# GpSimd adds the two key halves of the weights before the sums' product, and the residual one tick later

## The reference, cut to what matters

```python
x = x + _L2_attn_ref(_layernorm(x, axis=-1), ...)
qkv = data @ W_qkv + b_qkv
scores = jnp.einsum('nqhd,nkhd->nhqk', q, k)
attention = jax.nn.softmax(scores / jnp.sqrt(jnp.float32(HD)), axis=3)
out = jnp.einsum('nhql,nlhd->nqhd', attention, v).reshape(n, l, DIM)
return out @ W_out + b_out
```

## Time and profile before

| | before |
|---|---|
| median of 3 runs | 2783.32 us (2780.84 to 2787.41) |
| profiled execution | 2796.33 us |
| its span | 2794.7 us |
| PE busy | 2456.9 us, 88% |
| DVE busy | 1694.2 us, 61% |
| ACT busy | 1488.0 us, 53% |
| POOL busy | 1457.4 us, 52% |

### The profile page before, as it was taken

How to read it: one execution, slowest core, us unless ns; L and a number is a source line. 1 busy time by engine, 2 the same in 40 slices (tenths; PEclk the granted TensorE clock), 3 DMA queues, 4 the chain that set the end, 5 groups by cost and what they waited for, 6 DMA issues and landing times. The chain is left out here.

```text
span 2794.7 us, 62868 instructions
## 1 busy us (share of the span) xinstructions
PE 2456.9 (88%) x24585; PEld 1891.2 (68%) x24585; DVE 1694.2 (61%) x4435; ACT 1488.0 (53%) x3177; POOL 1457.4 (52%) x2282
## 2 busy tenths in 40 slices
PE   4999999999988688889998999999999676778855
PEld 3888888888876455557777777777777564445533
DVE  4677777777657477745444666666665215555557
ACT  3666666666644467744444555555555224555631
POOL 4787777777766444434332344444444126554454
PEclk9999999999999699999999999999999897999975
DMA  3790000000000100000000000000000440000000
GB/s 108 237 329 16 2 2 2 2 2 2 2 2 1 50 2 2 2 1 22 0 1 3 4 4 4 6 6 4 5 5 5 153 141 16 7 7 3 1 1 30
DMA packets 23255, 83.14 MB, mean 30 GB/s; under 512 B 4113, under 2 KB 11026, under 8 KB 21938
## 3 DMA queue, kind: packets, MB, share of 16 engines
q1 hardware_dynamic: 19810, 71.90, 7.9%
q0 software_dynamic: 3152, 7.21, 0.8%
HBM read 71.89 MB, written 46.79 MB: 42 GB/s over the span
## 5 line engine op out<-in xcount | busy, mean ns | idle before, releaser
L825 POOL TENSOR_TENSOR XR<-XR,T 128x256 f32<-128x256 f32 x512 | 375.9, 734 | 441.8 <-DVE T L708 411.7
L2416 PE MATMUL ps<-P,V 128*64 128x256 f32 (+3 forms) x4096 | 338.6, 353 | 14.4 <-DVE O L1270 12.3
L589 ACT ACTIVATE P<-ps 128x384 f32<-128x384 f32 (+1 forms) x512 | 250.7, 542 | 187.6 <-PE ps L2416 187.1
L1260 DVE TENSOR_REDUCE qa<-ps 128x2 fp32r<-128x512 f32 x256 | 176.4, 689 | 211.6 <-PE ps L2416 210.8
L1188 ACT ACTIVATE P<-ps 128x768 f32<-128x768 f32 x256 | 207.8, 812 | 147.9 <-PE ps L2416 146.6
L2416 PEld LDWEIGHTS ps<-P,V 128*64 128x64 f32 (+1 forms) x4096 | 187.1, 125 | 125.5 <-issue 25.6
L2416 PE MATMUL ps<-mk,identb 128*128 128x256 bf16 (+1 forms) x1024 | 199.5, 297 | 68.2 <-DVE qa L1261 65.3
L719 DVE TENSOR_REDUCE sm<-ps 128x2 f32<-128x512 f32 (+1 forms) x256 | 130.7, 552 | 179.2 <-PE ps L2416 178.4
L1350 POOL TENSOR_SCALAR_AFFINE_SELECT P<-P 128x512 f32<-128x512 f32 x256 | 163.2, 638 | 137.4 <-ACT P L1188 137.3
L836 POOL TENSOR_TENSOR ss<-ss,nhalf 128x16 f32<-128x16 f32 x64 | 187.8, 2935 | 5.3
L2416 PE MATMUL ps<-QH,KH 64*128 64x256 f32 (+1 forms) x1024 | 165.4, 314 | 8.6 <-DVE QL L677 0.6
(11 more groups left out here) (312 smaller groups left out, 7361.4 us busy)
## 6 DMA issues: line engine op xcount, KB each, us to landing
rows_i<-in_zero SPq DMA_DIRECT2D x16, 1208.0 KB, 31.6
rows_o<-in_zero SPq DMA_DIRECT2D x16, 1208.0 KB, 80.2
w<-in_m_w SPq DMA_DIRECT2D x23, 578.0 KB, 4.0
zt<-rows_i SPq DMA_DIRECT2D x23, 128.0 KB, 3.1
rows_o<-yo POOLq DMA_DIRECT2D x23, 128.0 KB, 3.9
stg<-in_t_w SPq DMA_DIRECT2D x11, 256.0 KB, 2.7
XR<-in_x SPq DMA_DIRECT2D x4, 512.0 KB, 8.5
out<-XR SPq DMA_DIRECT2D x8, 256.0 KB, 2.0
```

Source lines behind the costliest of these rows:

```text
L589: e.activation(self.P[at % 6][:, :], K.ps.ap("st", s, g, h)[:, 0:self.w], ACT.Exp, bias=0.0, scale=1.0 if kind == 0 else 0.125).then_inc(K ...
L825: p = po.e.tensor_tensor(x, x, self.T[g % 2][:, par, pr], ALU.add)
L1260: e.tensor_reduce(nm[:, 1], ps[:, :, 0:256], X, ALU.max, negate=True)
L2416: return self.te.matmul(o, l, r, start=start, stop=True, skip_group_check=True)
```

## The change

In kind 2, POOL adds the second half of the columns of each head's `P` to the first half, into one of eight new tiles `PS` of 128x256, two heads a tick, in the ticks of `st`. The product with ones then runs over `PS`: four products a unit in place of eight, each clearing its own strip. PE waits for the semaphore `halved` between the weighted values and the sums; ACT may write a buffer of `P` again when the weighted values are done and POOL has halved it, where it waited for the sums. `pool_sum` moves from k = 13 to k = 14, and `unit` from 14 to 15, so a unit has one more part and `Dispatch` starts one tick later. Kind 0 keeps its work.

```diff
-            first, last, unit = 6, 5, 14
+            first, last, unit = 6, 5, 15
...
+            self.PS = [sb(f"PS{s}_{i}", [128, 256], F32) for i in range(8)]
+            self.halved = K.sem(f"halved{s}")
...
-        for kt, q, c, w in self.blocks():
+        if kind == 2:
+            pe.wait_ge(self.halved, 4 * g + 4)
             for h in range(4):
-                p = K.acc(sm[32 * h:32 * h + 32, q:q + w], self.one[:, 0:32], P[h][:, c:c + w],
-                          start=kind == 2 and kt == 0)
+                p = K.acc(sm[32 * h:32 * h + 32, 0:256], self.one[:, 0:32], self.PS[(4 * g + h) % 8][:, :], start=True)
...
-                    ac.wait_ge(*K.ps.filled("sm", s, (at - 6) // 4))
+                    ac.wait_ge(*K.ps.filled("sm" if kind == 0 else "pv", s, (at - 6) // 4))
+                    if kind == 2:
+                        ac.wait_ge(self.halved, at - 5)
...
-                if self.part("out", k) is not None:
+                n = self.part("st", k)
+                if n is not None and self.kind == 2:
+                    self.pool_halve(po, 4 * a[0] + a[1], n)
+                if k == self.tk["out"] + (self.kind == 2):
                     self.pool_sum(po, *a)
...
+    def pool_halve(self, po, g, n):
+        K, s = self.K, self.s
+        for h in (2 * n, 2 * n + 1):
+            at = 4 * g + h
+            if at >= 8:
+                po.wait_ge(*K.ps.filled("sm", s, g - 2))
+            po.wait_ge(*K.ps.read("st", s, g, h))
+            P = self.P[at % 6]
+            po.e.tensor_tensor(self.PS[at % 8][:, :], P[:, 0:256], P[:, 256:512], ALU.add).then_inc(self.halved, 1)
```

More of the change, by code:

```diff
@@ L461, in pe_pv @@
         p.then_inc(K.ps.full_of("pv", s, g), 1)
-        for kt, q, c, w in self.blocks():
+        if kind == 2:
+            pe.wait_ge(self.halved, 4 * g + 4)
             for h in range(4):
-                p = K.acc(sm[32 * h:32 * h + 32, q:q + w], self.one[:, 0:32], P[h][:, c:c + w],
-                          start=kind == 2 and kt == 0)
+                p = K.acc(sm[32 * h:32 * h + 32, 0:256], self.one[:, 0:32], self.PS[(4 * g + h) % 8][:, :], start=True)
+        for kt, q, c, w in self.blocks() if kind == 0 else ():
+            for h in range(4):
+                p = K.acc(sm[32 * h:32 * h + 32, q:q + w], self.one[:, 0:32], P[h][:, c:c + w])
         p.then_inc(K.ps.full_of("sm", s, g), 1)
```

## The result

| | before | after |
|---|---|---|
| median of the runs | 2782.88 us (4 runs) | 2845.51 us (4 runs, 2841.1 to 2852.5) |
| profiled execution | 2796.33 us | 2848.57 us |
| stage, first product to the places of its last scatter | 662.1 us | 722.9 us |
| one sequence: gated unit, the next, two plain | 10.27 + 10.35 + 9.68 + 9.68 = 39.97 us | 14.81 + 10.94 + 9.30 + 9.31 = 44.37 us |

The gated unit is the one in four that carries a `prep` and a `Dispatch`. The ratio is 1.0221 [1.0207, 1.0235]: 62.6 us slower, where +34.8 was forecast. The stage itself is 60.8 us longer, so the loss lies in it. (The two profiled executions differ by only 52.2 us, because the one of before lies 13 us above its median.) The periods of the units are distances between the starts of their weighted values; 14 sequences x (44.37 - 39.97) = 61.6 us (the first of them is 0.8 shorter).

The account below looks back on a forecast made before the run. PE was taken to bound the kernel, busy 69.09 of 70 us. Terms: -27.5 + 60.5 + 1.8 = +34.8 us on the median 2783.3, forecast 2818 us; range 2782 to 2850.

Parts of the forecast that it names:

- What PE saves: PE's sums in each unit: 8 instructions in place of 16, 0.43 us less, 27.5 us over 64 units.
- The halving's cover: POOL's halvings, 0.79 us each, are hidden behind PE's weighted values of 1.88 us; no wait taken before the sums.
- The bank: Second scores product waits for banks read by QL and the reciprocal, late behind POOL's adds: PE loses 2.36 us, 14 times.
- The transposes of zd: PE, ready at 11.98 us, waits until 13.94 for DVE's zd, which now stands behind T, nm and KL.
- this unit loses 4.32 us: Unit where `prep` and `Dispatch` meet: next weighted values start at 14.16 us, not 9.84; 14 times, 60.5 us.
- the clock falls too: Rival: PE's granted clock falls after its waits, 1.62 us lost each; one at each of 14 places gives 2841; chance 0.18.
- b = 14: The sequence whose `Dispatch` meets no `prep`: adds early, only zd late, 1.8 us lost.
- the likeliest case: Whole kernel from 2808 to 2828 us, with each of the 14 losses between 3.6 and 5.0 us.
- one wait alone: Rival: only the bank's wait, net +5.5 us, 2789; or only zd's, net about -0.5 us, 2783; chance 0.13.

Follow-up runs that it names:

- work in both waits: Against the kernel after, in 14 sequences PE computes the values' product three times ahead of zd's transposes and the output product twice ahead of the bank wait; ratio 1.0169.

## Why the prediction was right in its direction and too low

- **What PE saves: right.** The sums take 0.64 us for 1.07. Plain units take 9.30 us for the forecast 9.25: scores wait 0.19 us for ACT in about half of the units, which the forecast had left out.
- **The halving's cover: right in this kernel, for less reason than given.** 731 ns each, where 0.79 us with its wait was taken from the add, and no wait for it. The argument looked at the exponentials alone; the kernel with the halving alone shows that the adds' place in POOL's queue decides it.
- **The bank: right.** Counted from the weighted values, the adds were to end at 6.52 us, QL to start at 7.45, the scores at 8.59; they did at 6.50, 7.35 and 8.41. The wait is 2.30 us, 2.36 was forecast.
- **The transposes of zd: right in place, too small.** KL was to end at 13.2 us and ended at 13.15. Then zd was priced at 0.59 from the earlier trace rows. In the moved place POOL runs adds of 128x256 beside it, and it takes 1.00: this is the first mis-sized term, 0.41 us a sequence, about 6 us. In the step "this unit loses 4.32 us", the operation kept the price of its old neighbours.
- **The clock: the second mis-sized term, and the larger one.** The forecast took no fall and gave "the clock falls too" a chance of 0.18. That rival is what happened, in addition to the forecast: 1.48 us a sequence was measured against the 1.62 that the rival had from the earlier trace rows. The choice rested on one row in which a wait of 2.03 us was followed by a clock of 1.00. That row excludes nothing: with the adds ahead of the roots this very wait has a fall behind it, and in the kernel with the early gate, waits of one length, 2.3 us, had one in 9 of 14 sequences.

The sum: a sequence was to take 39.97 - 4 x 0.43 + 4.32 = 42.57 us. Without falls it takes 42.89 (work in both waits): 0.41 more in the gated unit, as much as zd takes more, and 0.10 less in the other three. With falls it takes 44.37. The excess of 1.80 us x 14 is 25 us. For b = 14 the gated unit took 12.53 us where it took 9.90 before, 2.63 more where -0.43 + 1.8 = 1.37 was forecast, another 1.3 (the 15th wait for zd, 2.8 us). Together that is 26 of the 28 us between the forecast of 2818 and 2845.5. The measured time lies above the likeliest case, 2808 to 2828, and a little above the 2841 of the rival with one fall a sequence; it is inside the range because the range was drawn up to a fall at most places, not because the sum held.

The rival on the other side, one wait alone, has its two halves measured. With the wait for zd alone (the adds ahead of the roots) the ratio is 1.0066, where 2783 of 2783 was forecast; with the bank's alone (the gate a tick earlier) it is 1.0108, where 2789 was. In both the larger part of the difference is not the clock: without a fall a sequence takes 40.83 us where 40.05 follows from the forecast, and 41.89 where 40.61 does. The two instructions of zd take 1.65 and 1.24 us there, in place of 0.59, and what stands behind zd is late with it; no run separates the two. The falls add 6.0 us in all to the one kernel and 2.2 us to the other.

What stays open is when the clock falls. Both waits gave 14 falls in 14 sequences (after), the bank's alone 9 in 14, the bank's with that of zd cut to 1.1 us 10 in 14, that of zd alone 3 in 14, and both cut to 1.4 and 1.1 us none in 14; the wait at the stage's start had one in 1 of 10 traces. The runs give the price of a fall in each place, 0.05 to 1.63 us; they do not give a rule for when one comes.

## What to carry to other kernels

A part that is moved by one tick is moved in every engine's queue: write down, for each queue, what the moved instruction now stands behind and beside, and price it by its new neighbours, not by its row of before. Where a change makes a TensorE that was never idle wait two us once in a while, count the clock's fall in: here single waits of 2.3 and 2.6 us had one behind them at 9 and 3 of 14 places. What it costs depends on what stands in the slow stretch: here 1.5 us where the other engines stood waiting for PE, and 0.05 to 1 us where PE had waits for DVE left in it. And before giving up a change that saves on the busiest engine, look for the order in which its cover costs nothing: here the same halving was worth 1.0221 and 0.9912, by the order of the queues and one wait.

## What the runs showed of the hardware

DVE's zd, a `tensor_scalar` from SBUF to SBUF, takes 336 ns with POOL idle, and up to 878 ns beside POOL's adds of 128x256 (of a pair, one may still take 334); KL, which reads PSUM, keeps its 0.86 us for two beside the same adds. The Trainium skill (SBUF — State Buffer, Who interferes with whom) has DVE and GpSimd share one pair of ports, held for a whole instruction, and names `tensor_scalar` among the operations that can take it. The trace agrees: 336 against 724 ns in the median.

On the clock, waits of 2.3 and 2.5 us had a stretch at 1.2 GHz behind them, about three us long, in a stage whose other stretches ran at 2.4. The Trainium skill (TensorE: Matmul & The Clock Gate, Part 1: The HAM clock gate) says that throttled is the default and that activity releases it; the runs agree in that filling the waits with more products, 0 falls for 14, made the stage 18.1 us shorter.
